# Four of five layer norms applied on VectorE instead of ScalarE, with new orders and banks

## The chip, the cores and the metric

The kernel runs on one core of one Trainium2 chip. The metric is the device time of one execution in microseconds (us), lower is better. The engines are named as in the profile: PE (TensorE matmuls) and PEld (its weight loads), DVE (VectorE), ACT (ScalarE), POOL (GpSimd), SP (SyncE, which only issues DMAs here).

## What is computed

128 graphs, each with 128 nodes and 256 features, go through four graph layers, each followed by a residual and a layer norm:

```python
def _layernorm(x, axis=-1, eps=1e-05):
    m = jnp.mean(x, axis=axis, keepdims=True)
    v = jnp.var(x, axis=axis, keepdims=True)
    return (x - m) / jnp.sqrt(v + eps)
...
x = _layernorm(x + _L0_gnn_ref(x, adj, ...))            # neighbour mean
x = _layernorm(x + _L1_gnn_ref(x, adj, nodemask, ...))  # softmax over nodes
x = _layernorm(x + _L2_gnn_ref(x, adj, adj, ...))       # 8-head attention
x = _layernorm(x + _L3_gnn_ref(x, adj, ...))            # two hypergraph convolutions
```

The last layer has a fifth layer norm inside, over 512 features after a relu. In the kernel they are named ln0 (after layer 0), ln1, ln2, ln3 (the inner one, 512 wide) and ln4 (the output).

## The kernel before

A group is four graphs; a program of 32 groups runs as a software pipeline. One graph's nodes lie on the 128 partitions. Each engine has a written-out list of stages (`ORDER_TEXT`), walked once per group: `ln0_norm.2+` is stage `ln0_norm` of graph 2, and a `+` says that it works one group ahead. In the list for PE a number behind a colon is the PSUM bank. `FIRST_TEXT` is the prologue's list, `LAST_TEXT` the last group's. Nothing reorders at run time: an engine that waits in one stage holds up everything behind it in its list. All hand-overs are semaphores.

A layer norm of one graph is this chain: DVE takes the statistics (`bn_stats`, L1020) and aggregates them to mean and variance (`bn_aggr`, L1025, tile `ln_mv`); POOL adds epsilon (L878, `ln_ve`), raises to the power -1/2 (L880, `ln_rs`, the root) and multiplies the two to a shift, -mean x root (L883, `ln_nm`); ACT applies scale and shift in one activation (L718). Its result goes to PE (transposes and matmuls: `x1t`, `amx`, `x2t`, `tx`, `mn`) and, for ln1 and ln2, to POOL adds (`x2c`, `x3b`). The group has 20 norms: 4 each of ln0, ln1, ln2 and ln4 with 256 elements a partition, and 4 of ln3 with 512.

POOL further multiplies attention probabilities (`probs`, L900, 1024 elements a partition), adds biases (`xb` L890, `x2c` L895, `x3b` L963), makes `c3` in two operations of 1024 elements (L953, L956), and `amT` and `hb` (L912, L924, 512 elements). DVE adds, subtracts and reduces from PSUM; in the steady loop each of its operations reads at most one full tensor from SBUF. Many of its steps are the low half of a split (`x1t_lo` and others, L1035), which waits until ACT has cast the high half (L710).

Of the kernel before, what the change touches and what calls it, by code (L numbers as in the profile page):

```python
# [18 lines left out]
G = 4  # L19
# [35 lines left out]
        pt.2 x1t.2+ amx.1+ ln0_norm.3+ cx.2 amx.2+ ln2_norm.1 x1t.3+ hbc.0+ amx.3+ relu.0 pt.3 cx.3 tx.1
        wexp.0+ ln3_norm.0 ln2_norm.2 ln2_norm.3 tx.2 ln1_norm.0+ mn.0 ln1_norm.1+ relu.1 ln1_norm.2+ tx.3
        x2t.0+ ln1_norm.3+ x2t.1+ x2t.2+ x2t.3+ relu.2 relu.3 ln3_norm.1 q0.0+ k1.0+ q1.0+ ln3_norm.2 k0.0+
        mn.1 ln3_norm.3 ln4_norm.0 mn.2 mp.0+ exp0.0+ mn.3 mp.1+ exp1.0+ ln4_norm.1 exp0.1+ v2.0+ exp1.1+
        pt.0+ ln4_norm.2 ln4_norm.3
    """,  # L60
    "dve": """
        asum.0+ cx_lo.0 zmax0.2 zmax1.2 ax_lo.0+ hT.0+ wo.0 hT.1+ hT.2+ hT.3+ ax_lo.1+ ln2_stats.0
        ln2_aggr.0 h0.0+ drcp.0 ln0_stats.0+ h0.1+ ax_lo.2+ ln0_aggr.0+ z1.3 z0.3 ln0_stats.1+ h0.2+
# [33 lines left out]
        at.0+ ax.0+ at.1+ at.2+ at.3+ hi_w0.0+ ax.1+ ax.2+ ax.3+ gramhi.0+ ln0_norm.0+ hi_wv1.0+ gramhi.1+
# [1151 lines left out]
```

## Time and profile before

| | us |
|---|---|
| median of 3 runs | 1777.85 (1776.85 to 1778.46) |
| the profiled execution | 1777.09 |
| its span from first to last instruction | 1775.3 |
| PE busy | 1739.4 (98%) |
| PEld busy | 1564.2 (88%) |
| DVE busy | 1463.3 (82%) |
| ACT busy | 1454.2 (82%) |
| POOL busy | 1386.3 (78%) |

A busy time is the union of an engine's instruction spans. Matmuls are pipelined, so a busy PE is not PE at its peak. The granted TensorE clock is 0.999 over the span. DMA moves 35 GB/s and is idle for most of the span.

### The profile page before, as it was taken

Reading aid. Unit: us, or ns where it says so; the run is one execution under the profiler, and the core shown is the slowest. Engines: PE = TensorE matmul, PEld = TensorE weight load, DVE = VectorE, ACT = ScalarE, POOL = GpSimd, SP = SyncE. Lnnn points to the kernel's source line nnn. Section 1 sums busy time; section 2 is a strip of 40 time slices with the busy share of each in tenths; the row PEclk is TensorE's granted clock in tenths of the full one; section 3 lists DMA queues with packets and bytes.
Section 4 is the critical chain, followed back from the end, with each engine's and each line's share of the span. In section 5 each row is a group of like instructions: output and inputs, shape, how many; then the busy total and the mean of one; then the engine's idle time right before and its main releaser. Section 6 shows DMA issues by size and latency. Waiting matters only on the chain. (4 is left out here: it accounts for less than half of the span.)

```text
span 1775.3 us, 51999 instructions
## 1 busy us (share of the span) xinstructions
PE 1739.4 (98%) x15358; PEld 1564.2 (88%) x15358; DVE 1463.3 (82%) x4038; ACT 1454.2 (82%) x4463; POOL 1386.3 (78%) x2825
## 2 busy tenths in 40 slices
PE   7999999999999999999999999999999999999997
PEld 6888888889888898888898888988888988989886
DVE  7888888888888888888888888888888888888886
ACT  5888788888878887888888788878888887888786
POOL 4777778787788777787877887777878778777776
PEclk9999999999999999999999999999999999999999
DMA  4111101111001111011110011110111100111000
GB/s 130 31 43 42 33 18 32 41 41 37 20 25 41 41 41 33 16 34 41 41 36 21 27 41 41 41 32 17 34 41 41 33 23 27 41 41 41 27 6 22
DMA packets 93590, 62.94 MB, mean 35 GB/s; under 512 B 8430, under 2 KB 92924, under 8 KB 93564
## 3 DMA queue, kind: packets, MB, share of 16 engines
q1 hardware_dynamic: 92748, 61.58, 11.6%
q10 hardware_dynamic: 816, 1.05, 0.2%
q8 instruction: 12, 0.20, 0.1%
q14 instruction: 14, 0.11, 0.0%
HBM read 45.82 MB, written 16.78 MB: 35 GB/s over the span
## 5 line engine op out<-in xcount | busy, mean ns | idle before, releaser
L779 ACT ACTIVATE z<-z,z_max 128x128 f32<-128x128 f32 x1024 | 399.3, 397 | 5.4 <-DVE z_max L1119 3.9
L880 POOL TENSOR_TENSOR ln_rs<-ln_ve,minus_half 128x1 f32<-128x1 f32 x640 | 353.2, 552 | 50.0
L878 POOL TENSOR_TENSOR ln_ve<-ln_mv,eps_col 128x1 f32<-128x1 f32 x640 | 122.8, 192 | 178.7 <-DVE ln_mv L1025 175.8
L883 POOL TENSOR_SCALAR ln_nm<-ln_mv,ln_rs 128x1 f32<-128x1 f32 x640 | 171.2, 268 | 110.1 <-POOL ln_rs L880 109.9
L900 POOL TENSOR_TENSOR z<-z,z_rcp 128x1024 f32<-128x1024 f32 x128 | 243.0, 1899 | 8.7 <-DVE z_rcp L1126 5.5
L510 PE MATMUL ps<-w2T,mnT 128*128 128x256 f32 x1536 | 208.6, 284 | 0.0
L510 PE MATMUL ps<-w1T,txT 128*128 128x512 f32 x768 | 205.1, 404 | 0.1
L779 ACT ACTIVATION_READ_ACCUMULATOR z<-z,z_max 128x1 f32 x1024 | 198.2, 194 | 0.0
L510 PEld LDWEIGHTS ps<-w2T,mnT 128*128 128x128 f32 x1536 | 187.8, 188 | 4.2 <-DVE mnT L1035 0.4
L1035 DVE TENSOR_TENSOR mnT<-ps,mnT 128x512 fp32r<-128x512 f32 x128 | 86.8, 678 | 112.1 <-ACT mnT L710 112.0
L1119 DVE TENSOR_REDUCE z_max<-z 128x4 f32<-128x512 f32 x256 | 170.0, 675 | 0.1
L1108 DVE SCALAR_TENSOR_TENSOR z<-ps,a_hold 128x512 f32<-128x512 f32 x256 | 166.8, 682 | 0.7 <-PE ps L574 0.4
L510 PEld LDWEIGHTS ps<-w1T,txT 128*128 128x128 f32 x768 | 135.1, 189 | 22.6 <-DVE txT L1035 0.3
L615 PE MATMUL ps<-mp,h 128*128 128x128 f32 x1024 | 138.2, 278 | 0.3 <-ACT h L718 0.3
L786 ACT COPY pT<-ps 128x1024 f32<-128x1024 f32 x128 | 129.0, 1008 | 10.8 <-PE ps L583 10.8
L718 ACT ACTIVATE h<-h,ln_nm,ln_rs 128x512 f32<-128x512 f32 x128 | 103.9, 811 | 40.1 <-POOL ln_nm L883 40.1
L1025 DVE BATCH_NORM_AGGREGATE ln_mv<-ln_st 128x2 f32<-128x6 f32 x640 | 113.1, 177 | 27.7
L583 PE MATMUL ps<-ident,z 128*128 128x128 f32 x1024 | 134.9, 274 | 0.9 <-POOL z L900 0.8
L615 PEld LDWEIGHTS ps<-mp,h 128*128 128x128 f32 x1024 | 126.8, 191 | 6.6 <-ACT h L718 0.5
L718 ACT ACTIVATE x<-x2c,ln_nm,ln_rs 128x256 f32<-128x256 f32 x128 | 77.5, 606 | 61.2 <-POOL ln_nm L883 61.1
L510 PE MATMUL ps<-w,axT 128*128 128x256 f32 x768 | 126.5, 301 | 0.0
L510 PE MATMUL ps<-gram,x1T 128*128 128x256 f32 x768 | 126.3, 300 | 0.0
(154 smaller groups left out, 4928.9 us busy)
## 6 DMA issues: line engine op xcount, KB each, us to landing
x_in<-in_x_dram SPq DMA_DIRECT2D x128, 128.0 KB, 2.1
a_hold<-in_adj_dram SPq DMA_DIRECT2D x128, 128.0 KB, 2.2
out_dram<-y_out SPq DMA_DIRECT2D x128, 128.0 KB, 1.7
a_in<-in_adj_dram SPq DMA_DIRECT2D x128, 64.0 KB, 1.9
h<-in_L_gnn_W_dram SPq DMA_DIRECT2D x2, 512.0 KB, 7.3
x<-in_L_gnn_Wqk_dram ACTq DMA_DIRECT2D x1, 512.0 KB, 3.6
y_out<-in_L_gnn_W_dram ACTq DMA_DIRECT2D x1, 256.0 KB, 4.4
y_out<-in_L_gnn_Wv_dram ACTq DMA_DIRECT2D x1, 256.0 KB, 5.3
```

What stands on the lines that cost most here:

```text
L510: m = pe.matmul(o, left(i, c), right(j, c), start=(k == 0), stop=(k == len(passes) - 1))
L583: m = pe.transpose(ps[:, b + h // 4, (h % 4) * P:(h % 4 + 1) * P], z[:, g % 2, h, :], ident[:, :])
L615: m = pe.matmul(o[:, c * P:(c + 1) * P], h1[:, g, c * P:(c + 1) * P], mp[:, g, 0:P], start=True, stop=True)
L718: act.activation(dst(g), src(g), ACT.Identity, bias=nm[n][:, g:g + 1], scale=rs[n][:, g:g + 1]).then_inc(norm_made[n], 1)
L779: m = act.activation(z[:, g % 2, h, :], z[:, g % 2, h, :], ACT.Exp, bias=z_max[:, g % 2, h:h + 1], accum_out=z_sum[:, g % 2, h:h + 1])
L786: act.copy(pT[:, g % 2, :, :].rearrange("p (b h) n -> p b (h n)", b=2), ps[:, b:b + 2, :]).then_inc(read["pt"], 1)
L878: pool.tensor_tensor(ve[n][:, g:g + 1], mv[n][:, g, 1:2], (eps4_col if n == "ln4" else eps_col)[:, :], ALU.add).then_inc(eps_made[n], 1)
L880: pool.tensor_tensor(rs[n][:, g:g + 1], ve[n][:, g:g + 1], minus_half[:, :], ALU.pow).then_inc(root_made[n], 1)
L883: pool.tensor_scalar(nm[n][:, g:g + 1], mv[n][:, g, 0:1], rs[n][:, g:g + 1], -1.0, ALU.mult, ALU.mult).then_inc(shift_made[n], 1)
L900: pool.tensor_tensor(zg, zg, z_rcp[:, g % 2, :].unsqueeze(2).to_broadcast([P, HEADS, P]), ALU.mult)\
L1108: dve.scalar_tensor_tensor(out=z[:, g % 2, hs, :].rearrange("p (r c) n -> p r (c n)", r=RG // 2), in0=ps[:, b:b + RG // 2, 0:C * P], scala ...
L1119: dve.tensor_reduce(z_max[:, g % 2, hs], z[:, g % 2, hs, :], AX.X, ALU.max, negate=True)\
```

## The change

For ln0 to ln3 the stage `lnX_norm` leaves ACT's lists and enters DVE's: one `tensor_scalar`, (x - mean) x root, with both scalars read per partition from SBUF, and input and output in SBUF. It waits for the root instead of the shift, and POOL makes a shift for ln4 alone. ln4's norm stays on ACT. All orders and the PSUM banks are new; the set of stages on every engine is otherwise the same, PE's too.

```diff
 ORDER_TEXT = {
...
     "dve": """
...
-        ln1_aggr.0+ v1.2+ ln1_stats.1+ ln1_stats.2+ ln1_aggr.1+ ln1_aggr.2+ v1.3+ tx_lo.2 ln1_stats.3+ h1.1
...
+        tx_lo.3 ln1_aggr.3+ ln1_norm.1+ ln3_norm.0 h1.1 x2t_lo.0+ ln1_norm.2+ ln1_norm.3+ x2t_lo.1+ h1.2
...
     "pool": """
...
+        ln2_root.3 ln1_root.0+ ln1_root.1+ ln1_root.2+ ln1_root.3+ c3.0 ln3_root.1 x3b.0 x3b.1 ln3_root.2
...
-                "ln0_norm": norm("ln0", lambda g: xb[:, g, :], lambda g: x1[:, g, :], free1),
-                "ln1_norm": norm("ln1", lambda g: x1[:, g, :], lambda g: x2[:, g, :], free2),
-                "ln2_norm": norm("ln2", lambda g: x2c[:, g, :], lambda g: x3[:, g, :], free3),
-                "ln3_norm": norm("ln3", lambda g: h1[:, g, :], lambda g: h1[:, g, :], lambda q, g: None),
...
                     pool.tensor_tensor(rs[n][:, g:g + 1], ve[n][:, g:g + 1], minus_half[:, :], ALU.pow).then_inc(root_made[n], 1)
+                    if n != "ln4":
+                        return
                     pool.wait_ge(set_ident, 1)
...
-            def norm(n, src):
+            def norm(n, src, dst=None, free=()):
...
+                def scaled_by_root(q, g):
+                    dve.wait_ge(root_made[n], nth(q, g))
+                    for reader in free:
+                        after(dve, reader, before(q, g, G))
+                    dve.tensor_scalar(dst(g), src(g), mv[n][:, g, 0:1], rs[n][:, g:g + 1],
+                                      ALU.subtract, ALU.mult).then_inc(norm_made[n], 1)
```

Two places show what the new lists do. The first is DVE in the steady loop, around ln1 (`x1` to `x2`) and ln3 (`h1`). Before:

```order
L1025 BN_AGGR ln1_mv<-ln1_st 128x2 x2
L1080 SCALAR_TENSOR_TENSOR x1<-ps,p_col,x1 128x256
L1035 TENSOR_TENSOR txT<-ps,txT 128x256
L1020 BN_STATS ln1_st<-x1 128x6
L1137 SCALAR_TENSOR_TENSOR h1<-ps,d_inv,b1_all 128x512
L1025 BN_AGGR ln1_mv<-ln1_st 128x2
L1035 TENSOR_TENSOR mnT<-ps,mnT 128x512
L1020 BN_STATS ln3_st<-h1 128x6
L1035 TENSOR_TENSOR txT<-ps,txT 128x256
L1035 TENSOR_TENSOR x2T<-ps,x2T 128x2x128 x4
L1137 SCALAR_TENSOR_TENSOR h1<-ps,d_inv,b1_all 128x512 x2
```

Of the change, the same part of the program:

```order
L1015 TENSOR_SCALAR x2<-x1,ln1_mv,ln1_rs 128x256
L1026 TENSOR_TENSOR txT<-ps,txT 128x256
L1009 BN_AGGR ln1_mv<-ln1_st 128x2
L1015 TENSOR_SCALAR x2<-x1,ln1_mv,ln1_rs 128x256
L1015 TENSOR_SCALAR h1<-h1,ln3_mv,ln3_rs 128x512
L1128 SCALAR_TENSOR_TENSOR h1<-ps,d_inv,b1_all 128x512
L1026 TENSOR_TENSOR x2T<-ps,x2T 128x2x128
L1015 TENSOR_SCALAR x2<-x1,ln1_mv,ln1_rs 128x256 x2
L1026 TENSOR_TENSOR x2T<-ps,x2T 128x2x128
L1128 SCALAR_TENSOR_TENSOR h1<-ps,d_inv,b1_all 128x512
L1026 TENSOR_TENSOR x2T<-ps,x2T 128x2x128 x2
```

The norms of ln1 and of the first ln3 now stand between the split's low halves (`txT`, `x2T`), and two norms of ln1 follow each other. The second place is POOL at the end of the ln1 roots, in the steady loop. Before:

```order
L878 TENSOR_TENSOR ln1_ve<-ln1_mv,eps_col 128x1
L880 TENSOR_TENSOR ln1_rs<-ln1_ve,minus_half 128x1
L883 TENSOR_SCALAR ln1_nm<-ln1_mv,ln1_rs 128x1
L895 TENSOR_TENSOR x2c<-x2,c2_all 128x256 x2
L336 REGISTER_ALU
L963 TENSOR_TENSOR x3b<-x3,c3 128x256
L924 TENSOR_TENSOR hb<-hT,e_rcp 128x4x128
L336 REGISTER_ALU
L963 TENSOR_TENSOR x3b<-x3,c3 128x256
L878 TENSOR_TENSOR ln3_ve<-ln3_mv,eps_col 128x1
L880 TENSOR_TENSOR ln3_rs<-ln3_ve,minus_half 128x1
```

Of the change:

```order
L860 TENSOR_TENSOR ln1_ve<-ln1_mv,eps_col 128x1
L862 TENSOR_TENSOR ln1_rs<-ln1_ve,minus_half 128x1
L937 TENSOR_TENSOR c3<-bw_all,d_cnt 128x1024
L940 TENSOR_TENSOR c3<-c3,b2_all 128x1024
L860 TENSOR_TENSOR ln3_ve<-ln3_mv,eps_col 128x1
L862 TENSOR_TENSOR ln3_rs<-ln3_ve,minus_half 128x1
L335 REGISTER_ALU
L947 TENSOR_TENSOR x3b<-x3,c3 128x256 x2
L860 TENSOR_TENSOR ln3_ve<-ln3_mv,eps_col 128x1
```

The shift (`ln1_nm`) is gone, and behind the last ln1 root stand the two operations of `c3`, where `x2c` stood; the first two `x3b` stand behind the second ln3 root. Elsewhere in the new list `probs` stands behind the first root of ln0, and the second behind the first root of ln2.

## Rows read from the trace of the kernel before

**Rows 1.** Busy time of each engine in 500 to 1586.1 us, 20 groups.

```profile
core 0: us, PE busy (x) PEld busy (x) DVE busy (x) ACT busy (x) POOL busy (x), PEclk, DMA share, GB/s
500.00:1586.10 1086.10, 1076.10 (x9562) 970.73 (x9561) 903.28 (x2501) 902.97 (x2782) 862.97 (x1760) 1.00 0.11 34
```

**Rows 2.** One matmul a group: min/median/max duration, first and last start.

```profile
L538 PE MATMUL ps<-ident,p_row x32: 271/272/272, 25.7 to 1707.5; 128*128 128x128 f32 x32
```

**Rows 3.** What PE waited for, 500 to 1586.1 us.

```profile
engine line waited for: us in total, times, longest us
PE ps L526 <- ACT pT L786: 6.4, 20, 0.3
PE ps L563 <- DVE z L1108: 3.6, 20, 0.2
```

**Rows 4.** What DVE waited for, same stretch: first and last of seven.

```profile
DVE mnT L1035 <- ACT mnT L710: 71.4, 20, 3.6
...
DVE txT L1035 <- ACT txT L710: 5.1, 20, 0.3
```

**Rows 5.** ACT's norm groups, same stretch: busy, mean ns, idle before.

```profile
L718 ACT ACTIVATE h<-h,ln_nm,ln_rs 128x512 f32<-128x512 f32 x80 | 64.9, 811 | 24.6 <-POOL ln_nm L883 24.6
L718 ACT ACTIVATE x<-x2c,ln_nm,ln_rs 128x256 f32<-128x256 f32 x80 | 48.5, 606 | 37.7 <-POOL ln_nm L883 37.7
```

**Rows 6.** POOL's costly groups, same stretch: busy us, mean ns, idle before.

```profile
L880 POOL TENSOR_TENSOR ln_rs<-ln_ve,minus_half 128x1 f32<-128x1 f32 x400 | 220.7, 552 | 31.3
L900 POOL TENSOR_TENSOR z<-z,z_rcp 128x1024 f32<-128x1024 f32 x80 | 151.9, 1899 | 1.9
L883 POOL TENSOR_SCALAR ln_nm<-ln_mv,ln_rs 128x1 f32<-128x1 f32 x400 | 107.0, 268 | 68.6 <-POOL ln_rs L880 68.6
L878 POOL TENSOR_TENSOR ln_ve<-ln_mv,eps_col 128x1 f32<-128x1 f32 x400 | 76.7, 192 | 109.0 <-DVE ln_mv L1025 107.7
L963 POOL TENSOR_TENSOR x3b<-x,c 128x256 f32<-128x256 f32 x80 | 59.0, 738 | 0.0
...
L956 POOL TENSOR_TENSOR c<-c,b_all 128x1024 f32<-128x1024 f32 x20 | 48.3, 2415 | 1.6
L953 POOL TENSOR_TENSOR c<-bw_all,d_cnt 128x1024 f32<-128x1024 f32 x20 | 37.9, 1896 | 0.0
L912 POOL TENSOR_TENSOR amT<-aT,mask 128x512 f32<-128x512 f32 x20 | 20.8, 1042 | 0.0
```

**Rows 7.** Two groups of DVE with PSUM input, whole span.

```profile
L1087 DVE TENSOR_SCALAR hT<-ps 128x128 f32<-128x128 f32 x128 | 33.5, 284 | 12.9 <-ACT aT L710 12.9
L1131 DVE TENSOR_TENSOR x2c<-ps,x2c 128x256 f32<-128x256 f32 x128 | 54.0, 422 | 4.2 <-PE ps L510 1.7
```

**Rows 8.** Timeline, 39 to 43 us: start us, us, engine, line.

```profile
39.65 0.78 POOL L895 TENSOR_TENSOR x2c<-x,c_all 128x256 f32<-128x256 f32 x1
39.76 0.83 DVE L1173 TENSOR_SCALAR x<-c,cols 128x256 f32<-128x256 f32 x1
40.39 1.09 POOL L924 TENSOR_TENSOR hb<-hT,e_rcp 128x512 f32<-128x512 f32 x1
40.51 1.12 DVE L1173 TENSOR_SCALAR x<-c,cols 128x256 f32<-128x256 f32 x1
41.45 0.77 POOL L895 TENSOR_TENSOR x2c<-x,c_all 128x256 f32<-128x256 f32 x1
41.55 0.81 DVE L1173 TENSOR_SCALAR x<-c,cols 128x256 f32<-128x256 f32 x1
```

**Rows 9.** Timeline, 9 to 10 us: three DVE tensor_scalars back to back.

```profile
9.23 0.68 DVE L1087 TENSOR_SCALAR hT<-ps 128x128 f32<-128x128 f32 x3
```

**Rows 10.** The chain that ended last, near its end: start us, us.

```profile
1759.54 0.27 POOL ln_nm L883
1759.83 0.82 ACT h L718
```

More of the change, by code:

```diff
@@ L55 @@
[L55 to L59, printed above, removed]
+        at.0+ at.1+ cx.0 v2.3 at.2+ ax.0+ exp0.2 ax.1+ ax.2+ exp1.2 at.3+ mp.3 pt.1 ax.3+ x1t.0+ pt.2 cx.1
@@ L60 @@
+        cx.2 amx.0+ exp1.3 x1t.1+ exp0.3 x1t.2+ amx.1+ x1t.3+ amx.2+ hbc.0+ amx.3+ tx.0 pt.3 cx.3 relu.0
+        wexp.0+ tx.1 tx.2 tx.3 x2t.0+ x2t.1+ x2t.2+ x2t.3+ relu.1 relu.2 relu.3 mn.0 v2.0+ k1.0+ q0.0+ k0.0+
+        mn.1 q1.0+ mp.0+ mp.1+ mn.2 exp0.0+ exp1.0+ mn.3 v2.1+ exp0.1+ ln4_norm.0 exp1.1+ mp.2+ pt.0+
+        ln4_norm.1 ln4_norm.2 v2.2+ ln4_norm.3
     """,
     "dve": """
-        asum.0+ cx_lo.0 zmax0.2 zmax1.2 ax_lo.0+ hT.0+ wo.0 hT.1+ hT.2+ hT.3+ ax_lo.1+ ln2_stats.0
-        ln2_aggr.0 h0.0+ drcp.0 ln0_stats.0+ h0.1+ ax_lo.2+ ln0_aggr.0+ z1.3 z0.3 ln0_stats.1+ h0.2+
@@ L73 @@
+        ln4_aggr.0 zmax1.0+ z1.1+ z0.1+ y.1 zmax0.1+ zrcp.0+ mn_lo.3 ln4_stats.1 zmax1.1+ y.2 ln4_aggr.1
+        ln4_stats.2 y.3 ln4_aggr.2 ln4_stats.3 ln4_aggr.3 zrcp.1+ z1.2+ z0.2+ zmax0.2+
     """,
     "pool": """
-        xb.0+ probs.1 xb.1+ xb.2+ mask.0+ dmax.0 am.0+ xb.3+ ln2_root.0 ln0_root.0+ dinv.0 ln0_root.1+
-        probs.2 ln0_root.2+ ln2_root.1 ln0_root.3+ probs.3 c3.0 wm.0+ ln3_root.0 ln2_root.2 ln2_root.3
-        ln1_root.0+ ln1_root.1+ ln1_root.2+ ln1_root.3+ x2c.0+ x2c.1+ x3b.0 hb.0+ x3b.1 ln3_root.1 x3b.2
@@ L78 @@
-        ln3_root.2 x2c.2+ ln4_root.0 ln3_root.3 x3b.3 ln4_root.1 x2c.3+ probs.0+ ln4_root.2 ln4_root.3
+        xb.0+ xb.1+ xb.2+ x2c.1 mask.0+ ln0_root.0+ probs.2 ln0_root.1+ xb.3+ am.0+ ln0_root.2+ dmax.0
+        ln0_root.3+ x2c.2 ln2_root.0 probs.3 dinv.0 x2c.3 wm.0+ ln2_root.1 ln2_root.2 ln3_root.0 hb.0+
+        ln2_root.3 ln1_root.0+ ln1_root.1+ ln1_root.2+ ln1_root.3+ c3.0 ln3_root.1 x3b.0 x3b.1 ln3_root.2
+        ln3_root.3 x2c.0+ x3b.2 x3b.3 ln4_root.0 probs.0+ ln4_root.1 ln4_root.2 ln4_root.3 probs.1+
@@ L95 @@
+        xg.2+:2 amx.3+:1 xg.3+:6 turn.10+:5 turn.11+:4 turn.12+:0 mp.0+:1 wt.0+:3 v1.0+:6 v1.1+:7 pb.0+:1
+        turn.13+:4 v1.2+:5 turn.14+:0 v1.3+:3 turn.15+:2 x2t.0+:6 x2t.1+:7 x2t.2+:3 mp.1+:0 x2t.3+:5
+        turn.16+:4 turn.17+:7 turn.18+:1 turn.19+:0 q1.0+:5 k1.0+:3 k0.0+:1 q0.0+:4 v2.0+:6 mp.2+:0 sc0.0+:1
+        sc1.0+:3 v2.1+:6 c2.0+:5 sc0.1+:0 sc1.1+:6 bw.0+:3 v2.2+:5 sc0.2+:0 sc1.2+:3 pt.0+:6
     """,
     "act": """
[L97 removed]
@@ L113 @@
+        turnlo.19+ scale.0+ lo_wo.0+ scale.1+ scale.2+ scale.3+ z0.0+ zmax0.0+ z1.0+ zmax1.0+ z0.1+ zmax0.1+
+        z1.1+ zrcp.0+ c2lo.0+ zmax1.1+ bwlo.0+ lo_w2.0+ zrcp.1+ z0.2+ z1.2+ zmax0.2+
     """,
     "pool": """
-        xb.0+ xb.1+ mask.0+ xb.2+ am.0+ xb.3+ ln0_root.0+ ln0_root.1+ ln0_root.2+ ln0_root.3+ rep.0+ wm.0+
-        half.0+ ln1_root.0+ ln1_root.1+ ln1_root.2+ ln1_root.3+ x2c.0+ x2c.1+ rep.1+ x2c.2+ hb.0+ x2c.3+
-        probs.0+
+        mask.0+ xb.0+ xb.1+ xb.2+ xb.3+ am.0+ ln0_root.0+ ln0_root.1+ ln0_root.2+ ln0_root.3+ rep.0+ half.0+
@@ L118 @@
+        hb.0+ wm.0+ rep.1+ ln1_root.0+ ln1_root.1+ ln1_root.2+ ln1_root.3+ probs.0+ x2c.0+ probs.1+
     """,
     "sp": """
-        la.0+ lx.0+ la.1+ in_mask.0+ la.2+ la.3+ in_b0.0+ lx.1+ lx.2+ lx.3+ lh.0+ in_v.0+ lh.1+ in_vec.0+
-        lh.2+ in_k.0+ in_bias.0+ in_q.0+ in_w1.0+ in_o.0+ lh.3+ in_w2.0+
+        in_mask.0+ la.0+ la.1+ la.2+ la.3+ lx.0+ in_b0.0+ lx.1+ in_v.0+ lx.2+ lx.3+ in_vec.0+ in_q.0+
+        in_o.0+ lh.0+ lh.1+ in_k.0+ in_bias.0+ lh.2+ lh.3+ in_w2.0+ in_w1.0+
     """,
@@ L131 @@
     "act": """
-        mp.2 mp.3 v2.1 exp1.2 cx.0 exp0.2 pt.1 exp0.3 cx.1 exp1.3 v2.2 pt.2 v2.3 ln2_norm.0 cx.2 pt.3
-        ln2_norm.1 cx.3 tx.0 tx.1 ln2_norm.2 relu.0 ln2_norm.3 tx.2 relu.1 tx.3 ln3_norm.0 relu.2 ln3_norm.1
-        mn.0 relu.3 mn.1 ln3_norm.2 ln3_norm.3 mn.2 mn.3 ln4_norm.0 ln4_norm.1 ln4_norm.2 ln4_norm.3
+        exp0.2 cx.0 exp1.2 pt.1 exp0.3 exp1.3 pt.2 cx.1 mp.3 tx.0 cx.2 v2.3 pt.3 cx.3 tx.1 relu.0 tx.2
+        relu.1 relu.2 tx.3 mn.0 relu.3 mn.1 mn.2 mn.3 ln4_norm.0 ln4_norm.1 ln4_norm.2 ln4_norm.3
@@ L142 @@
     """,
     "pool": """
-        probs.1 dmax.0 dinv.0 probs.2 ln2_root.0 probs.3 ln2_root.1 c3.0 ln2_root.2 ln2_root.3 x3b.0
-        ln3_root.0 x3b.1 ln3_root.1 x3b.2 x3b.3 ln3_root.2 ln3_root.3 ln4_root.0 ln4_root.1 ln4_root.2
+        x2c.1 x2c.2 x2c.3 probs.2 ln2_root.0 probs.3 dmax.0 dinv.0 ln2_root.1 ln2_root.2 c3.0 ln2_root.3
+        ln3_root.0 x3b.0 ln3_root.1 x3b.1 ln3_root.2 x3b.2 x3b.3 ln3_root.3 ln4_root.0 ln4_root.1 ln4_root.2
         ln4_root.3
@@ L269, in build @@
         rs = {n: sb(f"{n}_rs", G) for n in LNS}
-        nm = {n: sb(f"{n}_nm", G) for n in LNS}
+        nm = {"ln4": sb("ln4_nm", G)}
         layout = ("turn", "gram", "c2", "bw")
@@ L720, in norm @@
                 return run
-            def free1(q, g):
-                after(act, made["x1t"], before(q, g, G))
-                after(act, made["amx"], before(q, g, G))
-                after(act, norm_made["ln1"], before(q, g, G))
-            def free2(q, g):
-                after(act, made["x2t"], before(q, g, G))
-                after(act, x2c_made, before(q, g, G))
-            def free3(q, g):
-                after(act, made["tx"], before(q, g, G))
-                after(act, x3b_made, before(q, g, G))
             def pairs(o):
@@ L1194, in _ @@
             plain = {}
-            plain.update(norm("ln0", lambda g: xb[:, g, :]))
-            plain.update(norm("ln1", lambda g: x1[:, g, :]))
-            plain.update(norm("ln2", lambda g: x2c[:, g, :]))
-            plain.update(norm("ln3", lambda g: h1[:, g, :]))
+            plain.update(norm("ln0", lambda g: xb[:, g, :], lambda g: x1[:, g, :], (made["x1t"], made["amx"])))
+            plain.update(norm("ln1", lambda g: x1[:, g, :], lambda g: x2[:, g, :], (made["x2t"], x2c_made)))
+            plain.update(norm("ln2", lambda g: x2c[:, g, :], lambda g: x3[:, g, :], (made["tx"], x3b_made)))
+            plain.update(norm("ln3", lambda g: h1[:, g, :], lambda g: h1[:, g, :]))
             plain.update(norm("ln4", lambda g: x3b[:, g, :]))
```

92 lines of the change are left out of this document (44 added, 48 removed).

## The prediction

> **What bounds the kernel now.** I read the page's busy shares first, then the same five engines over 20 groups in the middle of the span, then the waits of PE and of DVE there, then the groups of POOL, and last the timeline of the prologue, the only place where DVE now runs an operation of the new kind.
>
> One matmul that comes once a group starts first at 25.7 and last at 1707.5 us, 32 times [rows 2]: (1707.5 - 25.7) / 31 = 54.25 us a group, and in the steady part 1086.10 / 20 = 54.3 us [rows 1]. PE is busy for 1076.10 of 1086.10 us, 53.8 of 54.3 a group [rows 1], and what it lacks is two waits, 6.4 us for ACT's copy of pT and 3.6 us for a PSUM bank that DVE empties, together 0.50 us a group [rows 3]. So PE sets the pace, and the others matter only when they make PE wait or need more than 54.3 us a group themselves.
>
> DVE is busy 903.28 / 20 = 45.2 us a group [rows 1]. Its idle time is 9.1 us, and seven kinds of waits, all for ACT, make up 147.9 us of the stretch, 7.4 a group; the largest, 71.4 / 20 = 3.6 us, is for one cast of mnT [rows 4]. The other 1.7 us are gaps too short to be listed, between dependent operations; they go with the work. DVE thus needs 45.2 + 1.7 = 46.9 us and has 7.4 us to give. ACT is busy 45.1 and POOL 43.1 us a group [rows 1].
>
> **The change, part by part.** *ACT* loses 4 x 811 ns of ln3 and 12 x 606 ns of ln0 to ln2 [rows 5] (three groups of 80, one of which stands there; their means differ by 4 ns at most): 3.2 + 7.3 = 10.5 us, and falls to 34.6 us a group. It was not the bound, so this is worth at most PE's wait for pT, 6.4 / 20 = 0.32 us a group.
>
> *POOL* loses 16 of 20 shifts of 268 ns and the idle before each, 68.6 us / 400 = 0.17 us [rows 6]: 4.3 + 2.7 = 7.0 us. Its busy time becomes 43.1 - 4.3 = 38.9 us, 72% of a group.
>
> *DVE* gets 16 tensor_scalars. Without disturbance I price them from below by the one on PSUM: three take 0.68 us back to back [rows 9] where one is 284 ns [rows 7], so each holds the engine (0.68 - 0.28) / 2 = 0.20 us. It has 128 elements. The new one has 256, but the prologue has four of 256 from SBUF to SBUF, which end 0.15 us after they are released [rows 8], less than 256 elements at the slope of [rows 7] would take (422 - 284 = 138 ns for 128 more, so 276 ns). It must move two elements in the time of one, and 0.20 us is its price too; for 512 it is 0.20 + 0.14 = 0.34. Sum: 12 x 0.20 + 4 x 0.34 = 3.7 us, DVE at 50.6 us, and PE would still be the bound, with 3.7 us to spare.
>
> But the same rows show what such an operation pays beside a busy POOL. The tensor_scalar at 39.76 took 0.83 us and ended at 40.59, and POOL's add had ended at 40.43; the next ended at 41.63 where POOL's had ended at 41.48; the next at 42.36 where POOL's had ended at 42.22 [rows 8]. Three times, whatever POOL's length, 0.14 to 0.16 us behind it: DVE was held until POOL's operation was over, and POOL put one operation between each two of DVE's. In the loop before, no DVE operation shows this. The change puts 16 a group there, beside a POOL that is busy for 72% of the time.
>
> The Trainium skill says the same of the mechanism and gives it a reason: in "SBUF — State Buffer", section "Who interferes with whom", a VectorE operation in a two-port mode and a GpSimd operation hold a shared port pair exclusively, and the second one fully blocks. Its "VectorE: DVE Perf Modes" (the errata's measurements, fixed term about 150 cycles) would price the operations alone, an estimate of (128 + 150) / 0.96 = 290 ns and 423 ns, 5.2 us a group at full length, and by that PE stays the bound; the first page speaks against it, and the trace agrees with the first at 0.83 and 1.12 us.
>
> How long is the hold? Bounds first. *Below*: none, if every norm falls where POOL waits. *If the norms fall at random*: an operation of length d that runs n times a group adds n x d x d / 2. From [rows 6], with the counts a group: 20 roots of 552 ns 3.05; 4 probs of 1899 7.2; 20 of 192 0.4; 12 adds of 738 3.3; c3 2.9 and 1.8; amT and hb of 1042 1.1; sum 19.7, over 54.3 us a mean rest of 0.36 us. A held operation saves its start, 284 - 150 = 134 ns, in 72% of the cases, 0.10. So 0.27 us each, 16 x 0.27 = 4.3 us. *Above*: the new lists put long POOL operations right behind a root that a norm waits for: probs behind ln0's and ln2's first (1.9 each), c3 beside the last two of ln1 (1.9 and 2.4), x3b and x2c behind ln3's second and fourth (0.74 each), together 9.6 us, and the other ten at 0.27, 12.3 us a group. I take 4.3, the random value: several norms stand a few operations behind their root, and the queues shift against each other.
>
> DVE then needs 46.9 + 3.7 + 4.3 = 54.9 us, more than PE's 54.3. An engine that works its list in order is not free of waits even when it is the bound: of its 7.4 us a fuller DVE swallows the 3.6 us for mnT, and of the other 3.8 us of short waits I keep a third, 1.3. The period becomes 54.9 + 1.3 = 56.2 us, 1.9 over before, and over 31 periods +59 us. Behind DVE wait PE (banks that it empties, and now x1, x2, x3 and h1) and ACT (relu, exponentials).
>
> *The ends.* In the tail a shift of 0.27 us, its gap, and an activation of 0.82 us [rows 10] become one operation of about 0.4 us: -1 us. *Orders and banks* on PE hold the same matmuls; what they can bring is the 0.50 us of waits, and that is counted in a rival.
>
> Sum, against the profiled execution of 1777.09 us (span 1775.3; the median of the runs, 1777.85, is 0.8 above, which is nothing): 1777 + 59 - 1 = **1835 us**.
>
> **The rivals.** *1, faster: DVE still fits.* If the holds stay under 3.7 us a group, 0.23 us a norm, PE stays the bound, a relieved ACT no longer makes it wait for pT, and at best both waits go: 31 x 0.50 = 15.5 us, with the tail 1777 - 16 - 1 = 1760 us (1750 to 1773, since busy PE may hide short stalls). For it: the random value, 0.27, is only 0.04 above the point at which it decides, and POOL has long stretches of roots where it waits for DVE, 107.7 us in 20 groups [rows 6]. Against it: it needs DVE at 99% with no waits.
>
> *2, no change.* The operations fit, but the DVE wait of [rows 3] grows as much as ACT's goes: 1774 to 1781 us.
>
> *3, much slower: the holds cluster.* Norms wait for the root and then run straight into the long operation behind it. With half of the step to the upper bound, 8.3 us, the period is 46.9 + 3.7 + 8.3 + 1.3 = 60.2 us, +183 us, 1959 us; a quarter of the step gives 58.2 and 1897.
>
> *4, the operation is not a two-element one* with two scalars from SBUF. Then it isn't held, but costs 0.34 us for 256 elements and, by the slope of [rows 7], 0.34 + 0.28 = 0.62 for 512: 12 x 0.34 + 4 x 0.62 = 6.6, DVE at 53.5 us: within rivals 1 and 2.
>
> **How the numbers follow.** DVE becomes the bound, 0.62 in all, of it 0.10 for above 1895 us; its own range is 1790 to 1895. Rival 1 0.28, rival 2 0.10 (rival 4 is in these). A measurement of this kernel tells about 0.2% from no change, 3.6 us. Below 1758 us I leave 0.10, so the range is 1758 to 1895.
>
> **What would show it.** In the profile after: the DVE norm group with a mean well above 0.29 us (I expect 0.5 to 0.6 for 256 elements and 0.65 to 0.75 for 512), ends 0.15 us behind POOL's; ACT near 35 us and POOL near 39 us busy a group; DVE busy over 95% of a period and PE with listed waits for DVE's tiles of over 1 us a group. Wrong would be: a mean near 0.29 us, or PE still at 98 to 99% with a period of 54 us or less.

## The result and the profile after

The changed kernel took **2001.92 us** (median of 4 runs, 2001.57 to 2003.40), the kernel before 1778.15 us on the same chip (4 runs, 1776.85 to 1778.77): a ratio of 1.126 with an interval of 1.124 to 1.128, 224 us slower. The forecast, 1835 us, had the direction; its range ended at 1895.

The page of the changed kernel, engines first, then the chain that ended last:

```profile
PE 1824.5 (91%) x15358; PEld 1607.3 (80%) x15358; DVE 1812.0 (91%) x4550; ACT 1164.9 (58%) x3951; POOL 1285.7 (64%) x2313
...
PE 63%; DVE 29%; issue 7%; DVEq 1%; POOL 0%; ACT 0%; DMA 0%; SPq 0%; POOLq 0%
PE ps L509 33%; DVE x L1015 14%; PE ps L614 6%; PE ps L582 6%; PE ps L573 5%; DVE ln_st L1004 3%; PE ps L590 3%; PE ps L493 3%; DVE x L1071 2%; PE ps L562 2%; DVE ln_mv L1009 2%; DVE x2c L1122 1%; PE ps L603 1%; PE ps L547 1%; PE ps L525 1%
```

PE no longer works without a break, and the second entry of the chain by line is the new norm, L1015, with 14% of the span. The matmul that comes once a group [rows 2] and the busy times of 20 groups [rows 1] now read:

```profile
L537 PE MATMUL ps<-ident,p_row x32: 272/273/327, 28.5 to 1924.5; 128*128 128x128 f32 x32
```

```profile
core 0: us, PE busy (x) PEld busy (x) DVE busy (x) ACT busy (x) POOL busy (x), PEclk, DMA share, GB/s
500.00:1728.80 1228.80, 1130.01 (x9562) 997.53 (x9561) 1125.57 (x2821) 722.23 (x2462) 800.42 (x1441) 0.97 0.10 30
```

A group takes 1228.80 / 20 = 61.4 us, 7.1 more than before, and 31 x 7.1 = 221 of the 224 us are accounted for: the loss is in the loop, not at the ends. DVE is busy 56.3 us a group (45.2 before), ACT 36.1, POOL 40.0. The granted clock fell from 1.00 to 0.97.

The norms of these 20 groups, 80 of each layer norm (`x<-x` is ln1, `x<-x2c` ln2, `h<-h` ln3, `x<-xb` ln0), columns as in [rows 5]:

```profile
L1015 DVE TENSOR_SCALAR x<-x,ln_mv,ln_rs 128x256 f32<-128x256 f32 x80 | 94.1, 1196 | 0.0
L1015 DVE TENSOR_SCALAR x<-x2c,ln_mv,ln_rs 128x256 f32<-128x256 f32 x80 | 62.8, 786 | 7.1 <-POOL ln_rs L862 7.1
L1015 DVE TENSOR_SCALAR h<-h,ln_mv,ln_rs 128x512 f32<-128x512 f32 x80 | 58.7, 734 | 10.3 <-POOL ln_rs L862 8.8
L1015 DVE TENSOR_SCALAR x<-xb,ln_mv,ln_rs 128x256 f32<-128x256 f32 x80 | 58.0, 725 | 0.0
```

Together 273.6 / 20 = 13.7 us a group for 16 norms. Where it goes is seen in the timeline of DVE and POOL behind ln1's roots (start us, us, engine, line), in the group that starts at 511.39:

```profile
516.78 0.38 DVE L1015 TENSOR_SCALAR x<-x,ln_mv,ln_rs 128x256 f32<-128x256 f32 x1
517.08 0.54 DVE L1015 TENSOR_SCALAR h<-h,ln_mv,ln_rs 128x512 f32<-128x512 f32 x1
517.09 0.19 POOL L860 TENSOR_TENSOR ln_ve<-ln_mv,eps_col 128x1 f32<-128x1 f32 x1
517.36 0.66 POOL L862 TENSOR_TENSOR ln_rs<-ln_ve,minus_half 128x1 f32<-128x1 f32 x1
517.53 0.74 DVE L1128 SCALAR_TENSOR_TENSOR h<-ps,d_inv,b_all 128x512 f32<-128x512 f32 x1
517.99 1.89 POOL L937 TENSOR_TENSOR c<-bw_all,d_cnt 128x1024 f32<-128x1024 f32 x1
518.19 0.41 DVE L1026 TENSOR_TENSOR x2T<-ps,x2T 128x256 fp32r<-128x256 f32 x1
518.52 3.92 DVE L1015 TENSOR_SCALAR x<-x,ln_mv,ln_rs 128x256 f32<-128x256 f32 x2
519.96 2.34 POOL L940 TENSOR_TENSOR c<-c,b_all 128x1024 f32<-128x1024 f32 x1
...
552.17 1.90 POOL L884 TENSOR_TENSOR z<-z,z_rcp 128x1024 f32<-128x1024 f32 x1 [0.19 <-DVE z_rcp L1117]
552.53 1.69 DVE L1015 TENSOR_SCALAR x<-xb,ln_mv,ln_rs 128x256 f32<-128x256 f32 x1
```

The first two rows are norms alone: 0.38 and 0.54 us long, the next starts 0.30 and 0.45 us behind their start. The two norms of 518.52 meet the two operations of `c3` and take 3.92 us; they end at 522.44 where POOL ends at 522.30. The norm of 552.53 ends at 554.22, `probs` at 554.07. This is the mechanism of [rows 8], the same 0.15 us behind POOL in each of the 20 groups; the two held norms of ln3, with 512 elements, end 0.28 us behind it.

In the middle of the trace PE waits for the norms, and DVE for PE and ACT, as follows (us in total, times, longest us):

```profile
PE ps L547 <- DVE x L1015: 60.5, 40, 2.0
DVE mnT L1026 <- ACT mnT L709: 39.3, 40, 1.1
PE ps L520 <- DVE x L1015: 20.5, 20, 1.0
PE ps L603 <- DVE x L1015: 15.2, 20, 0.8
DVE h L1015 <- POOL ln_rs L862: 8.8, 20, 0.4
```

PE's three sum to 96.2 / 20 = 4.8 us a group, against 0.50 for its waits in [rows 3]. L547 transposes `x2`. The same group, cut where the granted clock changes, shows what follows from it (same columns as [rows 1]):

```profile
517.53:521.85 4.32, 1.96 (x10) 1.11 (x8) 4.32 (x5) 0.90 (x3) 4.24 (x3) 1.00 0.00 0
521.85:525.25 3.40, 2.75 (x13) 2.75 (x14) 3.34 (x7) 1.42 (x3) 0.45 (x1) 0.50 0.00 0
525.25:529.00 3.75, 3.75 (x20) 3.15 (x19) 2.56 (x7) 2.45 (x5) 2.15 (x4) 1.00 0.00 0
```

While the two norms are held, DVE reads as fully busy and PE works 1.96 of 4.32 us. Then, still within the hold, the granted clock falls to 0.50, the lower of its two levels (1.2 and 2.4 GHz), and stays there for 3.4 us, in 2.75 of which PE works. All 20 groups have one such stretch of 3.4 us; the rest of each reads 1.00. What it costs is read from e7 below.

### The profile page after: what moved, and what is told of

The parts are those of the page before. It is cut to its first block, busy times and chain, and to the rows that moved or that the text cites. A ratio compares the mean times of both kernels' runs of the same rounds, so it can differ in the third digit from the quotient of the medians.

```text
span 1999.4 us, 50875 instructions
## 1 busy us (share of the span) xinstructions
PE 1824.5 (91%) x15358; PEld 1607.3 (80%) x15358; DVE 1812.0 (91%) x4550; ACT 1164.9 (58%) x3951; POOL 1285.7 (64%) x2313
## 4 chain that ended last, share of the span: by engine, by line
PE 63%; DVE 29%; issue 7%; DVEq 1%; POOL 0%; ACT 0%; DMA 0%; SPq 0%; POOLq 0%
PE ps L509 33%; DVE x L1015 14%; PE ps L614 6%; PE ps L582 6%; PE ps L573 5%; DVE ln_st L1004 3%; PE ps L590 3%; PE ps L493 3%; DVE x L1071 2%; PE ps L562 2%; DVE ln_mv L1009 2%; DVE x2c L1122 1%; PE ps L603 1%; PE ps L547 1%; PE ps L525 1%
## 5 line engine op out<-in xcount | busy, mean ns | idle before, releaser
L862 POOL TENSOR_TENSOR ln_rs<-ln_ve,minus_half 128x1 f32<-128x1 f32 x640 | 374.8, 586 | 50.4
L765 ACT ACTIVATION_READ_ACCUMULATOR z<-z,z_max 128x1 f32 x1024 | 204.5, 200 | 0.0
L709 ACT CAST x2T<-ps 128x256 fp32r<-128x256 f32 x128 | 46.7, 373 | 189.9 <-PE ps L547 189.9
L614 PE MATMUL ps<-mp,h 128*128 128x128 f32 x1024 | 150.2, 295 | 0.3 <-DVE h L1015 0.3
L1015 DVE TENSOR_SCALAR x<-x,ln_mv,ln_rs 128x256 f32<-128x256 f32 x128 | 147.5, 1172 | 0.0
L614 PEld LDWEIGHTS ps<-mp,h 128*128 128x128 f32 x1024 | 145.1, 215 | 3.0 <-DVE h L1015 0.5
L547 PE MATMUL ps<-ident,x 128*128 128x128 f32 x256 | 60.0, 333 | 95.8 <-DVE x L1015 95.7
L1026 DVE TENSOR_TENSOR mnT<-ps,mnT 128x512 fp32r<-128x512 f32 x128 | 88.5, 691 | 61.5 <-ACT mnT L709 61.4
L509 PE MATMUL ps<-wvT,x2T 128*128 128x256 f32 x768 | 137.1, 328 | 1.1 <-DVE c_all L1156 0.8
L709 ACT CAST txT<-ps 128x256 fp32r<-128x256 f32 x128 | 47.1, 368 | 150.1 <-PE ps L603 150.1
L547 PEld LDWEIGHTS ps<-ident,x 128*128 128x128 f32 x256 | 31.5, 157 | 125.9 <-DVE x L1015 116.1
```

The lines of the kernel that those rows point to most:

```text
L509: m = pe.matmul(o, left(i, c), right(j, c), start=(k == 0), stop=(k == len(passes) - 1))
L547: m = pe.transpose(o[:, c * P:(c + 1) * P], x2[:, g, c * P:(c + 1) * P], ident[:, :])
L614: m = pe.matmul(o[:, c * P:(c + 1) * P], h1[:, g, c * P:(c + 1) * P], mp[:, g, 0:P], start=True, stop=True)
L765: m = act.activation(z[:, g % 2, h, :], z[:, g % 2, h, :], ACT.Exp, bias=z_max[:, g % 2, h:h + 1], accum_out=z_sum[:, g % 2, h:h + 1])
L862: pool.tensor_tensor(rs[n][:, g:g + 1], ve[n][:, g:g + 1], minus_half[:, :], ALU.pow).then_inc(root_made[n], 1)
L1015: dve.tensor_scalar(dst(g), src(g), mv[n][:, g, 0:1], rs[n][:, g:g + 1], ALU.subtract, ALU.mult).then_inc(norm_made[n], 1)
```

## The experiments

Each ran beside the kernel before on the same chip, which took 1776.79 to 1777.87 us there; one run each but for e10. "Group" is the distance of the matmul of [rows 2] over 20 groups in the middle, DVE and PE are busy us a group there, clock the granted one.

| kernel | us | group | DVE | PE | clock |
|---|---|---|---|---|---|
| before | 1778.15 | 54.3 | 45.2 | 53.8 | 1.00 |
| after | 2001.92 | 61.4 | 56.3 | 56.5 | 0.97 |
| e1 accumulator form | 1841.7 | 56.2 | 52.0 | 55.4 | 1.00 |
| e2 `c3` earlier | 2000.71 | 61.4 | 54.5 | 56.7 | 0.98 |
| e3 the norms back on ACT | 2108.27 | 64.9 | 44.8 | 58.2 | 0.95 |
| e4 `c3`, `probs` in pieces | 1824.84 | 55.7 | 50.9 | 54.8 | 1.00 |
| e5 e4, norms of 2 elements | 1786.43 | 54.4 | 48.8 | 54.1 | 1.00 |
| e6 only `c3` in pieces | 1884.02 | 57.6 | 53.4 | 55.2 | 1.00 |
| e7 only `probs` in pieces | 1937.34 | 59.2 | 53.7 | 55.8 | 0.98 |
| e8 before + 16 unread ones | 1894.66 | 57.9 | 50.8 | 56.1 | 1.00 |
| e9 old orders, 16 norms on DVE | 1934.64 | 59.4 | 51.1 | 56.3 | 1.00 |
| e10 old orders, ln3's 4 on DVE | 1794.99 | 54.9 | 46.8 | 54.4 | 1.00 |
| e11 before + 6 stats at a wait | 1778.19 | 54.3 | 47.1 | 53.8 | 1.00 |
| e12 before + 6 stats elsewhere | 1841.52 | 56.3 | 47.0 | 54.4 | 0.99 |

### e1_accum: the same norms in a form that is not held

```diff
-                                      ALU.subtract, ALU.mult).then_inc(norm_made[n], 1)
+                                      ALU.subtract, ALU.mult, accum_out=row_sum[n][:, g:g + 1]).then_inc(norm_made[n], 1)
```

> The changed kernel, same orders and banks, but each norm on DVE also writes out an accumulator, which should keep it at one element a cycle and away from POOL's port; everything else is as it was. Theory A (DVE is held by POOL's operations, and the loop pays for it): the norms lose their holds, none ends 0.15 us behind a long POOL operation; main operation 0.42 to 0.5 us for 256 elements and 0.7 to 0.8 for 512, plus a read of about 0.08. The period falls from 61.4 to 54.5 to 57 us, the time to 1785 to 1860 us. Theory B (the new orders and banks are slow by themselves): it stays above 1950 us.

1841.7 us, 160 less than after (this form changes what is applied to the values; operands and sizes are the same). Two of its four norm groups in the 20 groups:

```profile
L1017 DVE TENSOR_SCALAR_CACHE_REDUCE h<-h,ln_mv,ln_rs 128x512 f32<-128x512 f32 x80 | 64.2, 802 | 2.4
L1017 DVE TENSOR_SCALAR_CACHE_REDUCE x<-x,ln_mv,ln_rs 128x256 f32<-128x256 f32 x80 | 40.6, 526 | 0.0
```

ln1's, which averaged 1196 ns, are at 526, and all three groups of 256 elements lie within 526 to 530: none waits for POOL, though each costs 0.13 us more than an undisturbed norm of the change and is followed by a read of the accumulator of 0.08 us. A dearer operation in the same place made a kernel that is 160 us faster, within the range expected of theory A. The Trainium skill ("SBUF — State Buffer", section "Who interferes with whom") says just this, that `tensor_scalar` can contend with GpSimd, but not in the form that writes its accumulator; the rows agree.

### e2_c3_early: the long operations moved

```diff
-        ln2_root.3 ln1_root.0+ ln1_root.1+ ln1_root.2+ ln1_root.3+ c3.0 ln3_root.1 x3b.0 x3b.1 ln3_root.2
+        ln2_root.3 c3.0 ln1_root.0+ ln1_root.1+ ln1_root.2+ ln1_root.3+ ln3_root.1 x3b.0 x3b.1 ln3_root.2
```

> The changed kernel with one stage of POOL's steady list moved: c3 stands ahead of the four ln1 roots, not behind them. Theory A: the norms of ln1 of graphs 2 and 3, 1.51 and 2.50 us now, take 0.4 to 0.6, which takes 3 us off the loop: period 58 to 59.5, time 1900 to 1940 us. Theory B: c3's place doesn't matter, within 10 us of 2002; or it gets slower, since c3 now delays the ln1 roots by up to 4.3 us.

2000.71 us: nothing gained, and theory A's 1900 to 1940 us is refuted. The number is the one of theory B, but not since the place doesn't matter. The timeline:

```profile
513.28 1.89 POOL L937 TENSOR_TENSOR c<-bw_all,d_cnt 128x1024 f32<-128x1024 f32 x1
...
513.75 1.57 DVE L1015 TENSOR_SCALAR x<-x2c,ln_mv,ln_rs 128x256 f32<-128x256 f32 x1
...
515.25 2.39 POOL L940 TENSOR_TENSOR c<-c,b_all 128x1024 f32<-128x1024 f32 x1
...
517.86 0.55 POOL L862 TENSOR_TENSOR ln_rs<-ln_ve,minus_half 128x1 f32<-128x1 f32 x1
...
518.45 0.41 DVE L1015 TENSOR_SCALAR x<-x,ln_mv,ln_rs 128x256 f32<-128x256 f32 x1 [1.93 <-POOL ln_rs L862]
```

ln1's norms are now free (408 ns in the mean), but `c3` holds the last norm of ln2 for 1.57 us, and the second half of it delays the root of ln1, for which DVE waits 1.93 us. DVE is 1.8 us a group less busy and just as late. In this place 4.3 us of POOL stand between `x1` and `x2` whichever norm they hit.

### e3_act_norms: the new orders without the move

The norms of the loop went back into ACT's list, at places of my choosing, with their shifts on POOL:

```diff
-        at.0+ at.1+ cx.0 v2.3 at.2+ ax.0+ exp0.2 ax.1+ ax.2+ exp1.2 at.3+ mp.3 pt.1 ax.3+ x1t.0+ pt.2 cx.1
+        at.0+ at.1+ cx.0 v2.3 at.2+ ax.0+ exp0.2 ax.1+ ax.2+ exp1.2 at.3+ mp.3 ln0_norm.0+ pt.1 ax.3+ x1t.0+ pt.2 cx.1
...
```

> The changed kernel with its new orders and banks, but in the steady list the 16 norms of ln0 to ln3 are back on ACT (placed one or two stages ahead of their readers), and POOL makes all shifts again. Prologue and last group stay as changed. Theory A: about as before the change, period 54.3 to 57, 1780 to 1860 us. Theory B: still above 1950 us.

2108.27 us, with DVE waiting 285.8 us over the span for ACT's cast of mnT (61.4 after). By its number theory B holds, "above 1950", but that wait is one for ACT, in a list to which I added 16 norms at places that may be bad: the run can't tell whether the new orders are bad or these places. e5 and e9 bound that from two other sides.

### e4_split, e6_split_c3, e7_split_probs: long operations in pieces of 256

```diff
-                pool.tensor_tensor(c3[:, :, :], bw_all[:, :].unsqueeze(1).to_broadcast([P, G, D]),
-                                   d_cnt[:, :].unsqueeze(2).to_broadcast([P, G, D]), ALU.mult).then_inc(c3_half, 1)
+                for k in range(G):
+                    m = pool.tensor_tensor(c3[:, k, :], bw_all[:, :], d_cnt[:, k:k + 1].to_broadcast([P, D]), ALU.mult)
+                m.then_inc(c3_half, 1)
```

The second operation of `c3` and `probs` (two heads at a time) are cut alike in e4; e6 cuts `c3` alone, e7 `probs` alone. The work is the same, and POOL does more instructions.

> The changed kernel with POOL's operations of 1024 elements in four pieces of 256 each (probs and both of c3). POOL's busy time grows by 2 to 4 us a group, and it has 19 idle. Theory A: no norm is held for more than one piece, 0.7 us: the five longest (1.2 to 2.5 us) fall to 0.6 to 0.9, which takes 4 to 5 us off: period 57 to 58.5, 1865 to 1915 us. A rival, that the norms are slow by themselves or DVE is short of time whatever POOL runs: no change or slower, 2000 to 2060.

> The changed kernel with only the two operations of c3 in pieces of 256. Holds add up along DVE's list: the two ln1 norms lose 0.7 and 1.8 us, 2.5 of the 5.76 us that e4_split gained a group: 1920 to 1930 us. If holds are hidden in part behind each other (e2_c3_early gained nothing when the same two norms lost 3.2 us), 1960 to 2000.

> The changed kernel with only probs in pieces of 256. By the sum along DVE's list, the first norms of ln0 and ln2 lose 1.26 and 1.28 us, 2.5 us a group: 1920 to 1930 us, and with e6_split_c3 the two gains add up to 170 to 177 us. If only one of the two chains binds, one of these runs gains nearly all and the other nearly nothing.

e4 took 1824.84 us: 177 of the 224 us are gone, with POOL busier (42.8 for 40.0 us a group). That is theory A's direction and 40 us beyond its range; the rival is refuted. ln1's and ln0's norms there:

```profile
L1019 DVE TENSOR_SCALAR x<-x,ln_mv,ln_rs 128x256 f32<-128x256 f32 x80 | 43.6, 565 | 0.0
...
L1019 DVE TENSOR_SCALAR x<-xb,ln_mv,ln_rs 128x256 f32<-128x256 f32 x80 | 32.7, 409 | 0.0
```

ln0's mean is the undisturbed 0.40 us. e6 gave 118 us, more than expected (1920 to 1930 us), e7 65, less than expected; together 182 where both at once gave 177. e7's norms lost 2.5 us a group and its period 2.3; e6's lost 2.8 (ln1 from 1.17 to 0.54 us over the span, ln3 from 0.73 to 0.66) and its period 3.8. The times add up, but not because each hold counts in full: a part is the granted clock, and e7 shows it by itself. Seven of its 20 groups run at the full clock, the other 13 have the 3.4 us at the low level that every group of the changed kernel has. Two neighbours, cut at the matmul of [rows 2] (columns of [rows 1]):

```profile
853.01:911.17 58.16, 54.79 (x481) 48.62 (x480) 53.60 (x142) 35.84 (x123) 41.55 (x85) 1.00 0.10 32
911.17:970.96 59.79, 56.42 (x481) 49.90 (x479) 53.68 (x142) 35.99 (x123) 41.53 (x85) 0.97 0.10 31
```

The second is 1.6 us longer. The norms have the same lengths in both kinds of group, DVE is as busy, PE is 1.6 us busier with the same matmuls, and DVE waits 2.5 us for mnT where it waits 1.1. Over e7's groups the low stretch costs 1.4 to 1.6 us, and in e2, where 3 of 20 groups are free of it (60.27 us for 61.6), 1.3. At the same low clock e7's groups take 59.7 us against 61.4 after: 1.8 us for 2.5 us of holds. An estimate from these two runs is that 31 x 1.3 to 31 x 1.6, 40 to 50 of the 224 us, come by way of the clock, and they come with the holds: in e1, e4 and e6, where the two long holds at `c3` are gone, none of the 20 groups has the low level.

### e5_tiny: e4 with norms that cost next to nothing

```diff
-                    dve.tensor_scalar(dst(g), src(g), mv[n][:, g, 0:1], rs[n][:, g:g + 1],
+                    dve.tensor_scalar(dst(g)[:, 0:2], src(g)[:, 0:2], mv[n][:, g, 0:1], rs[n][:, g:g + 1],
```

> The kernel of e4_split (changed kernel, POOL's long operations in pieces), and the 16 norms on DVE touch 2 of their 256 or 512 elements: the rest of the normalisation is left out, every wait and every order stays. Theory A (what is left over the time before, 47 us in e4_split, is the norms' own time on DVE): the norms fall from 0.32 and 0.46 us of DVE to about 0.1, 4 us a group less, and PE is the bound again: period 53.4 to 54.4, time 1750 to 1785 us. Theory B (the new orders and banks cost it): it stays within 10 us of 1825.

1786.43 us, with all but two elements of each norm left out, 1.4 us above the range of theory A and far from B. Of the 47 us that e4 leaves, 38 go with the norms' own time. What remains, 9 us, is the net of everything else: the new orders, banks and ends, short holds, and the 0.2 us that a shortened norm still takes. And the timeline, in the place that was shown of after:

```profile
522.72 2.33 POOL L940 TENSOR_TENSOR c<-bw_all,d_cnt 128x256 f32<-128x256 f32 x4
523.00 0.93 DVE L1019 TENSOR_SCALAR x<-x,ln_mv,ln_rs 128x2 f32<-128x2 f32 x2
```

Two norms of two elements a partition take 0.93 us together; a single undisturbed one takes 0.25 us. A hold does not need a long operation on DVE.

### e8_dummy: the kernel before, plus the 16 operations, unread

```diff
+                    if n != "ln4":
+                        dve.wait_ge(extra_made, 1)
+                        after(dve, extra_made, q * 16 + (-8 if n in ("ln0", "ln1") else 8) + 1)
+                        dve.tensor_scalar(extra[:, LNS.index(n), g, :], ones_row[:, :], minus_half[:, :], eps_col[:, :],
+                                          ALU.subtract, ALU.mult).then_inc(extra_made, 1)
```

They stand behind the aggregates of ln0 to ln3, in the orders of before; ACT and POOL do all their old work.

> The kernel before, orders and all, with one added operation of the new kind behind each aggregate of ln0 to ln3 on DVE: 16 tensor_scalars a group of 256 elements, SBUF to SBUF with two scalars, on scratch that nobody reads. Nothing waits for them but what is queued behind them on DVE. Theory A: 16 x 0.32 = 5.1 us plus holds of 3 to 6 us go onto DVE's 46.9: period 56 to 59, 1830 to 1930 us, and their mean is well above 0.4 us. Rival (a DVE at 86% takes them in its 7.4 us of waits): within 1% of 1778.

1894.66 us. Three of 16 are held (0.74, 0.97 and 1.25 us long, behind `amT`, `probs` and `c3`). DVE gets 5.6 us busier a group, to 50.8, the period 3.6 us longer, to 57.9: DVE never gets near 57.9 of work. It still waits for mnT, 54.7 us in 20 groups where it was 71.4 [rows 4]. The holds are 1.8 us a group, less than the 3 to 6 expected. For this loss, 118 us, no root, no relieved ACT and no new order is needed.

### e9_old_order and e10_ln3_only: the move in the old orders

```diff
-        ln2_aggr.0 h0.0+ drcp.0 ln0_stats.0+ h0.1+ ax_lo.2+ ln0_aggr.0+ z1.3 z0.3 ln0_stats.1+ h0.2+
+        ln2_aggr.0 h0.0+ drcp.0 ln0_stats.0+ h0.1+ ln2_norm.0 ax_lo.2+ ln0_aggr.0+ z1.3 z0.3 ln0_norm.0+ ln0_stats.1+ h0.2+
...
-        y.0 ln3_stats.2 ln3_stats.3 ln3_aggr.2 ln3_aggr.3 ln4_stats.0 ln4_aggr.0 mn_lo.1 z0.0+ z1.0+
+        y.0 ln3_stats.2 ln3_norm.1 ln3_stats.3 ln3_aggr.2 ln3_aggr.3 ln4_stats.0 ln4_aggr.0 ln3_norm.2 mn_lo.1 ln3_norm.3 z0.0+ z1.0+
```

e9 moves all 16 in the loop, e10 the four of ln3; POOL makes all shifts in both.

> The kernel before with its own orders and banks, and in the steady list the 16 norms of ln0 to ln3 moved from ACT to DVE, one to four stages behind their aggregates; POOL still makes all shifts. The move without the new orders. Theory A (the move itself costs, by load and holds): period 57 to 62, 1860 to 2010 us. Theory B (the new orders are the fault): near 1778, at most 1800.

> The kernel before with its own orders, and only the four norms of ln3 moved to DVE in the steady list. DVE needs 46.9 + 4 x 0.46 + about 1.2 of holds = 49.9 us, well under 54.3; ACT loses 3.2 us. Theory A: no slower, 1765 to 1785 us. Rival: the place in the list costs more than the load, since a norm that waits for its root stops all of DVE: 1790 to 1830.

e9: 1934.64 us with one held norm a group. The norms are near their own price (547, 541, 410 and 408 ns in the mean for ln1, ln3, ln0 and ln2), and what is late now is a root:

```profile
DVE mnT L1042 <- ACT mnT L710: 46.9, 20, 2.4
DVE x L1031 <- POOL ln_rs L880: 46.3, 100, 0.8
PE ps L510 <- DVE txT L1042: 26.6, 20, 1.3
```

DVE waits 46.3 / 20 = 2.3 us a group for roots, where ACT before took the norm later in its list and DVE went on. The time is in theory A's range. e10: 1794.99 us (4 runs; ratio 1.010, 1.008 to 1.012), which is the rival's range and not theory A's "no slower". Four norms of 0.54 us, none held:

```profile
L1031 DVE TENSOR_SCALAR h<-h,ln_mv,ln_rs 128x512 f32<-128x512 f32 x124 | 66.8, 538 | 4.7 <-POOL ln_rs L880 3.4
```

Even this smallest part costs 0.6 us a group, for 1.65 us of work on a DVE that is busy 46.8 of 54.9 us, and with 2.6 us taken off ACT.

### e11_pad_wait and e12_pad_busy: the same 2 us in two places

Six `bn_stats` on a constant row, 0.41 us each and never held, once a group in the kernel before; in e11 ahead of the mnT operation that waits 3.6 us for ACT, in e12 in the stretch of the attention scores.

```diff
-        y.0 ln3_stats.2 ln3_stats.3 ln3_aggr.2 ln3_aggr.3 ln4_stats.0 ln4_aggr.0 mn_lo.1 z0.0+ z1.0+
+        y.0 ln3_stats.2 ln3_stats.3 ln3_aggr.2 ln3_aggr.3 ln4_stats.0 ln4_aggr.0 pad.0 mn_lo.1 z0.0+ z1.0+
```

```diff
-        zmax0.0+ mn_lo.2 y.1 ln4_stats.1 zmax1.0+ ln4_aggr.1 z0.1+ mn_lo.3 zmax0.1+ zrcp.0+ z1.1+ y.2
+        zmax0.0+ mn_lo.2 y.1 ln4_stats.1 zmax1.0+ ln4_aggr.1 z0.1+ mn_lo.3 zmax0.1+ pad.0 zrcp.0+ z1.1+ y.2
```

> The kernel before with six extra statistics operations of 256 elements on DVE a group, on a constant tile that nobody else uses: about 6 x 0.34 = 2.0 us of DVE, of a kind that POOL has never held. They stand directly ahead of the low half of mnT that waits 3.5 us for ACT. If DVE's waits are free room at their own place, nothing changes: 1774 to 1783 us. If DVE's time costs wherever it is spent, 1800 us or more.

> The same six operations in the stretch of the attention scores, behind the second zmax0, about 7 us behind that wait, where DVE has no wait of over 0.15 us ahead of it for 13 us. DVE's need is 48.9 us in both runs. If the sum over a group decides, as the prediction has it, 1774 to 1785 us here too. If the place decides, the 2 us are late for their readers: some 0.5 to 1.5 us a group, 1795 to 1825 us.

1778.19 and 1841.52 us: nothing, and 64 us. The wait for mnT over the whole span, in e11, then in e12, and below it the wait that PE gets in the 20 groups of e12:

```profile
DVE mnT L1037 <- ACT mnT L712: 50.3, 33, 1.7
```

```profile
DVE mnT L1037 <- ACT mnT L712: 111.6, 33, 3.6
...
PE ps L512 <- DVE x3b L1151: 30.3, 20, 1.5
```

In e11 the padding went into the wait. In e12, 16 us above the range expected of the place, the wait is as long as it ever was, PE waits 1.5 us a group for DVE, and the period grows by 2.04 us. Of this 0.3 us is the clock: five of the 20 groups have the low stretch and take 57.2 us, the other 15 take 56.1, 1.8 over before, where 6 x 0.33 = 2.0 us were added. DVE's work is the same in both runs, 47.1 and 47.0 us a group.

No version here beat the kernel before.

## Why the forecast was half right

**What was right.** A norm from SBUF to SBUF is held until POOL's operation ends (0.15 us behind, as in the prologue's rows); this was shown by leaving the form (e1, -160 us) and by cutting POOL's operations (e4, -177 us). ACT at 36.1 and POOL at 40.0 us came out near the 34.6 and 38.9 of the forecast. PE waits for DVE's tiles over 1 us a group, as the text asked. Two of its signs missed: DVE is busy for 56.3 of 61.4 us, 92% and not over 95%, and the norms of 256 elements average 0.73 to 1.20 us and not 0.5 to 0.6 (those of 512, 0.73, are in their range). Rivals 1 and 2 fell on it, and rival 4 did too, since the norms are held.

**The step that failed first: the length of the hold.** I had both numbers, 4.3 us a group for norms at random places and 12.3 by the new lists, and took the first, "several norms stand a few operations behind their root, and the queues shift against each other". They don't shift: the norm beside `c3` starts 0.52 to 0.53 us behind it in every one of the 20 groups. The six norms that the upper bound named are the six that are held (two of ln1 by `c3`, two of ln3 by `x3b` and `x2c`, one each of ln0 and ln2 by `probs`), and the other ten pay next to nothing. The holds are 13.7 - (12 x 0.40 + 4 x 0.545) = 6.7 us a group, where those six were bounded at 9.6. A list that runs in order, against another such list with semaphores between them, meets it at the same place each time; the mean over random arrivals is the wrong model. Of rival 3 the mechanism is what happened, at a chance of 0.10 too low.

**The second: the price of an undisturbed norm.** The prediction had 0.20 us, from an operation on 128 elements with two constants and PSUM input, and 0.34 for 512; the trace has 0.30 and 0.45 from start to start. Sixteen of them are 12 x 0.30 + 4 x 0.45 = 5.4 us, 5.6 with the small differences between them, instead of 3.7, and they count in full where DVE is waited for: e5, which makes them short, gave 38 us.

**The third: DVE's waits as room.** The text set 46.9 + 3.7 + 4.3 us against PE's 54.3 and kept 1.3 us of waits. Measured are 76.6 / 20 = 3.8 us of listed waits (seven kinds; the two largest on DVE stand above), and e11 and e12 show why the sum is the wrong test: 2 us are free at the one wait and cost 64 us somewhere else, with a DVE of 47 busy us in a group of 54 to 56. The chain of the changed kernel passes through PE (63%) and DVE (29%), and time on DVE counts where it does. In the orders of before, too, e8, e9 and e10 all got slower by a third to nine tenths of what DVE was given, with no engine full.

**The sum, again.** Forecast 56.2 us, measured 61.4: holds +2.4, own price +1.9, waits +2.5 (1.3 to 1.6 of it comes with the clock's fall, by e2 and e7; the prediction had no term for the clock), and -1.7 in the rest of DVE's work and short gaps, which I took over unchanged at 46.9. Of that the other operations' durations account for 0.4 us (51.5 for 51.9 a group in sum) and unlisted gaps for 0.4 (1.3 for 1.7); the rest stays open.

**From the runs,** of the 224 us: long holds and what hangs on them, the low clock too, 177 (e4), the norms' own time 38 (e5), all else 9 net. Orders and banks of their own are in the 9; whether they alone would be good or bad stays open, since e3 didn't answer it, and a norm on DVE in the orders of before (e9, +158) is not as bad as with the new ones (+224).
